# First cross attention: the value products of four key chunks stand in one group in place of two, with eight buffers of exponentials in place of four

## The reference, cut to what matters

```python
def mha(q, k, v):
    qh = q.reshape(B, Sq, 16, 8).transpose(0, 2, 1, 3)      # Sq = 56
    kh = k.reshape(B, Skv, 16, 8).transpose(0, 2, 1, 3)     # Skv = 1500
    vh = v.reshape(B, Skv, 16, 8).transpose(0, 2, 1, 3)
    scores = jnp.einsum('bhqd,bhkd->bhqk', qh, kh) / math.sqrt(8)
    attn = jax.nn.softmax(scores, axis=-1)
    return jnp.einsum('bhqk,bhkd->bhqd', attn, vh).transpose(0, 2, 1, 3).reshape(B, Sq, 128)

qkv = x @ w_qkv + b_qkv                                     # first layer
q, k, v = jnp.split(qkv, 3, axis=-1)
x = layer_norm(x + mha(q, k, v) @ w_so + b_so, ln_g, ln_b)
qc, kc, vc = x @ w_q + b_q, y @ w_k + b_k, y @ w_v + b_v    # y is the context
x = layer_norm(x + mha(qc, kc, vc) @ w_co + b_co, ln_g, ln_b)
x = layer_norm(x + ff(x), ln_g, ln_b)                       # three dense layers
# then the second layer: a wider cross attention over the same context
```

## Time and profile before

| what | value |
|---|---|
| median of three runs | 1087.92 us (1087.25 to 1088.80) |
| profiled execution | 1085.93 us, span 1084.1 us |
| PE, PEld busy over the span | 1009.3 us (93%), 736.4 us (68%) |
| DVE, ACT, POOL busy over the span | 742.8 us (69%), 566.5 us (52%), 377.6 us (35%) |
| the stretch of 13 batches, 122.60 to 416.70 us | 294.10 us |

### The profile page before, as it was taken

One profiled execution on the slowest core, in us unless ns is written; L12 is line 12 of the kernel. 1 busy time (PEld: TensorE's weight loads), 2 busy tenths in 40 slices (PEclk: granted clock), 3 DMA queues, 4 the chain that ended last, 5 costly groups with the idle time before them and its releaser, 6 DMA issues. The chain is left out here.

```text
span 1084.1 us, 31631 instructions
## 1 busy us (share of the span) xinstructions
PE 1009.3 (93%) x12044; PEld 736.4 (68%) x12044; DVE 742.8 (69%) x1409; ACT 566.5 (52%) x1135; POOL 377.6 (35%) x273
## 2 busy tenths in 40 slices
PE   6847999999999999888779999999999999999997
PEld 3633677777777777646327777777777777777786
DVE  5748887788877887212786767767677677767752
ACT  3623777777767776532434444434454453444542
POOL 6512111211112113020106554545556444555542
PEclk9977999999999999979799999999999999999998
DMA  3514444434454332210020122111011211102100
GB/s 126 123 43 124 131 148 145 139 121 132 142 149 134 120 113 72 67 35 1 7 69 28 55 57 59 54 38 55 22 56 55 57 44 47 45 32 57 35 4 4
DMA packets 47021, 79.90 MB, mean 74 GB/s; under 512 B 6978, under 2 KB 33812, under 8 KB 46964
## 3 DMA queue, kind: packets, MB, share of 16 engines
q1 hardware_dynamic: 46964, 79.11, 24.8%
HBM read 50.93 MB, written 21.96 MB: 67 GB/s over the span
## 5 line engine op out<-in xcount | busy, mean ns | idle before, releaser
L1385 ACT ACTIVATE P<-PS 125x448 f32<-125x448 f32 x384 | 207.1, 544 | 265.0 <-PE PS L1294 263.1
L1275 POOL TENSOR_TENSOR Pl<-P 125x896 f16<-125x896 f32 x128 | 229.9, 1801 | 237.0 <-ACT P L1385 237.0
L1021 DVE TENSOR_REDUCE m<-PS 128x1 f32<-128x500 f32 x336 | 220.8, 675 | 114.8 <-PE PS L1012 112.9
L927 DVE TENSOR_REDUCE m_part<-PS 128x1 f32<-128x500 f32 x336 | 210.4, 673 | 60.4 <-PE PS L829 58.9
L1310 PE MATMUL PS<-cNh,P 125*128 125x97 f16 x1344 | 197.9, 208 | 0.1
L1312 PE MATMUL PS<-cNh,Pl 125*128 125x97 f16 x1344 | 197.4, 207 | 0.0
L1311 PE MATMUL PS<-cNl,P 125*128 125x96 f16 x1344 | 196.8, 206 | 0.0
L905 ACT ACTIVATE Pb<-PS 125x448 f32<-125x448 f32 x384 | 186.0, 547 | 19.7 <-PE PS L804 18.7
L1311 PEld LDWEIGHTS PS<-cNl,P 125*128 125x128 bf16 x1344 | 131.9, 98 | 25.4
L829 PE MATMUL PS<-KH,Qmx 128*128 128x500 f16 x336 | 129.5, 388 | 14.3 <-PEq L701 8.2
L1310 PEld LDWEIGHTS PS<-cNh,P 125*128 125x128 bf16 x1344 | 131.2, 98 | 15.7 <-issue 3.2
(11 more groups left out here) (167 smaller groups left out, 1484.3 us busy)
## 6 DMA issues: line engine op xcount, KB each, us to landing
Kst<-k_halves SPq DMA_DIRECT2D x144, 125.0 KB, 2.8
k_halves<-KH SPq DMA_DIRECT2D x16, 750.0 KB, 3.3
cx<-in_ctx SPq DMA_DIRECT2D x16, 562.5 KB
d_cx<-in_ctx SPq DMA_DIRECT2D x16, 562.5 KB
c_halves<-cHi SPq DMA_DIRECT2D x16, 281.2 KB, 2.7
c_halves<-cLo SPq DMA_DIRECT2D x16, 281.2 KB, 3.1
cTh<-c_halves SPq DMA_DIRECT2D x16, 281.2 KB, 3.1
cTl<-c_halves SPq DMA_DIRECT2D x16, 281.2 KB, 4.0
```

Source lines behind the costliest of these rows:

```text
L927: nc.vector.tensor_reduce(m_part[:, t, part:part + 1], PS[:, 6 + k % 2, 0:SP], AX.X, ALU.max).then_inc(s_reduced, 1)
L1021: nc.vector.tensor_reduce(m21[:, t, part:part + 1], PS[:, S1[k % 2], 0:SP], AX.X, ALU.max).then_inc(n_red, 1)
L1275: nc.gpsimd.tensor_tensor(Pl[:, c % NP], P1[:, c % NP], high, ALU.subtract).then_inc(n_low_p, 1)
L1385: nc.scalar.activation(P1[:, c % NP, half * HALF:(half + 1) * HALF], PS[0:KC, u % 3, 0:HALF], ACT.Exp).then_inc(n_exp, 1)
```

## The change

The body of PE issues the value products at c = 5, 9 and 13, those of chunks c - 5 to c - 2 in one group, where it issued those of two chunks at c = 3, 5, 7, 9, 11 and 13. Pb holds eight chunks in place of four. Nothing else is edited: the same matmuls run, in another order on PE; ACT's and DVE's instructions keep their order, and ACT's wait at L904 is for chunk c - 8.

```diff
-        NPB = 4
+        NPB = 8
+        GV = 4
         LAG0 = 2
...
-                        if has_b and c % 2 == 1 and c >= LAG0 + 1:
-                            values(i, par, c - LAG0 - 1)
-                            values(i, par, c - LAG0)
+                        if has_b and c >= LAG0 and (c - LAG0) % GV == GV - 1:
+                            for k in range(c - LAG0 - GV + 1, c - LAG0 + 1):
+                                values(i, par, k)
```

## The result

The changed kernel took 1111.71 us (median of four runs, 1111.29 to 1117.45) against 1088.36 us for the kernel before: 1.0221 times as long, with a 95% interval from 1.0197 to 1.0246 (the ratio is estimated from all the runs; the two medians alone give 1.0215). Forecast was 1113 us, between 1103 and 1121, slower.

The account below looks back on a forecast made before the run. PE sets the pace, but its order hangs on DVE's ends. Batches 0 to 13 lose 23.8 us, batch 14 0.9, batch 15 0.4: +25.1 on the profiled 1085.93, 1111.0; runs' median 2.0 higher, so 1113 us, range 1103 to 1121.

Parts of the forecast that it names:

- What a group costs: Value products on PE: two chunks 1.00 us, four 1.77, switch 0.23; three groups fewer per batch save 0.69 us.
- Turns 3 to 8: PE waits for DVE at key pieces 0, 1, value piece 0, turned attention, piece 17: 0.35, 0.30, 0.26, 0.15, 0.34 us.
- piece 17: Turn 8: PE's piece 17 waits for DVE's reduction 15, 0.34 us, and starts 0.16 us late.
- DVE's wait for piece 19: Turns 9 to 11: DVE waits some 1.9 us for piece 19 in place of 1.26.
- Turns 9 to 11 and the last group: Piece 19 comes 0.93 us late, PE waits for the turned maximum, turn 13's group is 0.77 longer: 1.70 us a batch.
- the wait of 0.91: Turn 11: PE, free at 278.73, waits until 279.64 for the turned maximum, 0.91 us.
- the walk: Step through one loop batch with old clock times; the next batch begins 1.70 us later than before.
- The sum: Batches 0 to 13 lose 14 x 1.70 = 23.8 us, batch 14 0.9, batch 15 0.4: together +25.1 us.
- the 0.9 and 0.4: Losses taken for batch 14 (between 0.1 and 1.7 us) and batch 15 (from -0.46 to +1.0 us).
- The faster one: Rival: saved PE switches are all that counts, 10.6 us less, 1077 us; chance 0.07.
- The milder one: Rival: DVE's waits in turns 3 to 8 don't show, only turns 11 and 13: 1092, up to 1100 us; chance 0.13.
- The clock: Rival: clock falls to half for one 3.4 us stretch in each of 14 batches, 24 us more, 1137; chance 0.05.

Follow-up runs that it names:

- experiments with halved reductions: DVE's score-piece reductions over 250 of 500 columns: kernel before 1073.12 us, changed kernel 1074.44 us, changed kernel with turned maximum ahead of last group 1060.74 us.
- the third experiment: Against the kernel before, only the two earlier merges (groups of four at turns 5 and 9; two at 11 and 13): 1099.88 us, ratio 1.0115.
- the version with halved reductions and the turn moved: Changed kernel, DVE's score-piece reductions over 250 of 500 columns, turned maximum moved from turn 11 to 13 ahead of the last group: 1060.74 us.

## Why the prediction was right

**What a group costs** held: a group of 64 matmuls takes 1.74 in each of the rows shown, and from piece 10 to key piece 2 it is 280.95 - 278.97 - 0.21 = 1.77. The experiments with halved reductions show that the switch is a cost that can be saved.

**Turns 3 to 8** held within 0.02 us at four of the five waits. The term that was mis-sized is piece 17, 0.34 forecast and 0.26 measured: DVE starts reduction 15 at 285.51, before the normalising's last row has ended, while I let it start at that end. Beneath it lies a misreading that the sum does not show: I took the 0.33 us from the turned attention to piece 17 for the turned attention's own time, and 0.26 of it was a wait for reduction 15 in the kernel before as well. As the 0.33 stands on both sides, it drops out of the loss. DVE's wait for piece 19 is 2.04 us for some 1.9.

**Turns 9 to 11 and the last group** held: the wait of 0.91 to the second digit (with the 0.71 of the prediction for the scores ahead of it), and the experiments split the 1.70 as the walk did, 0.93 up to piece 19 (0.90 measured) and 0.77 behind it (0.77).

**The sum** held: 25.1 us forecast, 25.5 in the span. Batch 0 lost 1.8, batches 14 and 15 the 0.9 and 0.4 that were set for them; those two were set inside wide bounds and not worked out, so that they met to a tenth is luck. The 0.5 ahead of the first scores and 0.2 behind the last copy were not in the sum. The difference of the medians is 23.4: the runs of both kernels spread by some us, and the profiled execution of the kernel before lay 2.4 under their median, that of the changed one 0.4.

**Rivals.** The faster one would have come true with faster reductions and the maximum moved; in this kernel DVE's ends decide. The milder one falls with the third experiment, in which only the merges at turns 5 and 9 are left and the loss of those turns stands in full. The clock did not move in the stretch with PE busy 92% of it. The reason given for that does not carry, though: the prediction took 90% to be far from the one fall that it had seen, and in one of the experiments it fell to half at the end of a stretch with 3.18 of 3.40 us busy (last section). That the clock stayed is what this trace shows, and no more.

With DVE's reductions out of PSUM shorter by 0.25 us each, the same order of PE loses nothing. The Trainium skill, TensorEngine Tiling (Array Packing), section PSUM Bottleneck, names the evacuation of PSUM as what may bound instead of TensorE; the halved reductions agree with that rule. Whether it is the reading of PSUM or the reduction itself that takes DVE's time, no run here separates.

## What to carry to other kernels

A switch that can be saved is worth its price only where the instruction it stood before is ready earlier: before merging two groups on an engine that runs in order, write down for each instruction that moves up the end of what it waits for. Here bunched work on PE starved DVE, which is fed through two PSUM banks and was idle nearly a fifth of the time anyway: its wait for piece 19 went from 1.26 to 2.04 us. The better use of the same freedom was to put the movable work where the engine waits already, and to keep the last group ahead of a hand-over short, but not shorter than what it covers.

## What the runs showed of the hardware that was not expected

The turned maximum has 14 columns and writes to PSUM partitions 96 to 109, one strip of 32. Ahead of a group of products it stands in their way less than by itself: in the version with halved reductions and the turn moved, its first pass starts in the same 10 ns as the group's first products, which by the program go to other strips, and its second pass between them.

```profile
282.90 0.28 PE L849 MATMUL PS<-tab,mneg 128*14 128x128 f32 x1
282.90 0.30 PE L816 MATMUL PS<-Pb,Vst 125*32 125x112 f32 x3
283.01 0.27 PE L849 MATMUL PS<-tab,mneg 128*14 128x128 f32 x1
283.02 1.80 PE L816 MATMUL PS<-Pb,Vst 125*32 125x112 f32 x61
284.75 0.60 PE L805 MATMUL PS<-Qst,Kst 110*125 110x224 f16 x4
```

From the turned maximum to the scores behind the group that is 1.85 us. In the changed kernel the group by itself takes 1.68:

```profile
268.99 1.74 PE L816 MATMUL PS<-Pb,Vst 125*32 125x112 f32 x64
270.67 0.60 PE L805 MATMUL PS<-Qst,Kst 110*125 110x224 f16 x4
```

So it adds 0.17 us there, where by itself it takes 0.32 to the next start (278.71 to 279.03 in the kernel before). How much of the 0.19 us that three switches did not explain this is was not measured apart.

In the same run the granted clock fell to half, the lower of its two levels, in the last batch (columns as in the earlier trace rows):

```profile
410.20:413.60 3.40, 3.18 (x20) 1.47 (x22) 0.00 (x0) 3.40 (x9) 0.00 (x0) 0.97 0.00 0
413.60:417.00 3.40, 3.40 (x68) 3.07 (x68) 0.00 (x0) 0.82 (x2) 0.00 (x0) 0.53 0.02 5
```

PE was busy 3.18 of 3.40 us in the stretch at whose end it fell, and in the next stretch after these the clock was 1.00 again; the other profiled runs kept the full clock through that batch. Why it fell here was not tried.
